# Decoder layer on one core: gate parts in one operand, windowed slot sums, offsets read a tile ahead, low parts moved to GpSimd

## What is computed

```python
x = x + self_attention(layernorm(x), Wq, Wk, Wv, Wr)        # 16 heads of 64, causal mask of -50
x = x + cross_attention(layernorm(x), ctx, w_q, w_k, w_v, w_o)
x = x + ffn(layernorm(x), w_in, w_out, w1, w2, wg, we, gb, eb)

# ffn, flat = [2048, 256]
shared = (silu(a) * b) @ w_out.T            with a, b = split(flat @ w_in.T)      # 512 each
g_probs = softmax(flat @ wg.T + gb)         # 2 groups, the likelier one is taken
e_probs = softmax over the 4 experts of that group of (flat @ we.T + eb)
topv, topi = top_k(e_probs * g_prob, 2)     # two experts per token
h = silu(a1) * b1                           with a1, b1 = split(flat @ w1.T)
out = shared + sum over the two experts e of weight_e * (h @ w2[e].T)
```

## Time and profile before

| what | us |
| --- | --- |
| median of 3 runs (741.8 to 742.43) | 741.85 |
| the profiled execution | 741.35 |
| its span in the profile | 739.6 |
| TensorE busy | 732.7 |
| VectorE busy | 459.8 |
| ScalarE busy | 443.6 |
| GpSimd busy | 309.3 |

### The profile page before, as it was taken

One profiled execution on the slowest core, in us unless ns is written; L12 is line 12 of the kernel. 1 busy time (PEld: TensorE's weight loads), 2 busy tenths in 40 slices (PEclk: granted clock), 3 DMA queues, 4 the chain that ended last, 5 costly groups with the idle time before them and its releaser, 6 DMA issues.

```text
span 739.6 us, 17762 instructions
## 1 busy us (share of the span) xinstructions
PE 732.7 (99%) x6371; PEld 641.1 (87%) x6371; DVE 459.8 (62%) x951; ACT 443.6 (60%) x1473; POOL 309.3 (42%) x336
## 2 busy tenths in 40 slices
PE   8999999999999999999999999999999999999998
PEld 7888888888888888888888888888878889999987
DVE  6777767767667865564565555456767746444277
ACT  5876566665666778765656666657834534555322
POOL 2655225222423657363253226324660772445400
PEclk9999999999999999999999999999999999999999
DMA  6799600000000012000000000200050555777271
GB/s 200 239 372 203 229 1 0 0 0 0 0 0 1 29 63 82 2 29 3 1 0 28 0 0 17 96 0 2 30 228 1 200 200 176 236 210 210 69 274 66
DMA packets 35962, 64.68 MB, mean 87 GB/s; under 512 B 7972, under 2 KB 15652, under 8 KB 35332
## 3 DMA queue, kind: packets, MB, share of 16 engines
q1 hardware_dynamic: 31188, 50.17, 22.0%
q0 software_dynamic: 4432, 13.54, 4.9%
q10 hardware_dynamic: 288, 0.26, 0.1%
HBM read 38.06 MB, written 30.09 MB: 92 GB/s over the span
## 4 chain that ended last, share of the span: by engine, by line
PE 98%; ACT 0%; DVE 0%; POOL 0%; issue 0%; POOLq 0%; DVEq 0%
PE psW L150 15%; PE psW L152 14%; PE psW L151 14%; PE psW L927 8%; PE psT L913 5%; PE psT L150 4%; PE psT L152 4%; PE psT L151 4%; PE psS L981 4%; PE psA L981 4%; PE psS L150 4%; PE psS L152 3%; PE psS L151 3%; PE psA L152 2%; PE psA L151 2%; PE psA L150 2%
## 5 line engine op out<-in xcount | busy, mean ns | idle before, releaser
L530 POOL TENSOR_TENSOR prob<-prob,rsum 128x512 f32<-128x512 f32 x128 | 134.7, 1054 | 284.2 <-DVE rsum L777 284.2
L633 ACT ACTIVATE prob<-psA,nmin 128x128 f32<-128x128 f32 x256 | 91.8, 384 | 1.3
L633 ACT ACTIVATE prob<-psS,nmin 128x128 f32<-128x128 f32 x256 | 90.4, 376 | 1.9 <-DVE nmin L772 1.9
L608 ACT ACTIVATE oT_hi<-psW 128x512 fp32r<-128x512 f32 x63 | 37.7, 598 | 88.2 <-PE psW L927 88.2
L604 ACT ACTIVATE pT<-psT 128x512 f32<-128x512 f32 x64 | 38.3, 599 | 52.9 <-PE psT L913 52.0
L777 DVE RECIPROCAL rsum<-psums 128x4 f32<-128x4 f32 x128 | 21.9, 171 | 68.3 <-ACT prob L633 68.1
L927 PE MATMUL psW<-pT,v 128*64 128x128 f32 x1008 | 62.3, 276 | 0.0
L760 DVE COPY kt<-psW 128x512 f32<-128x512 f32 x57 | 39.3, 689 | 36.3 <-PE psW L152 36.3
L927 PEld LDWEIGHTS psW<-pT,v 128*64 128x64 f32 x1008 | 54.4, 137 | 6.6 <-issue 3.1
L753 DVE TENSOR_TENSOR oT_lo<-psW,oT_hi 128x512 fp32r<-128x512 f32 x63 | 43.2, 686 | 26.0 <-ACT oT_hi L608 25.8
L633 ACT ACTIVATION_READ_ACCUMULATOR prob<-psA,nmin 128x1 f32 x256 | 57.6, 225 | 0.0
(11 more groups left out here) (388 smaller groups left out, 2186.5 us busy)
## 6 DMA issues: line engine op xcount, KB each, us to landing
stage<-hs SPq DMA_DIRECT2D x39, 257.0 KB, 3.0
hs<-empty SPq DMA_DIRECT2D x1, 9984.0 KB, 35.3
w_lo<-w_raw SPq DMA_DIRECT2D x4, 1024.0 KB, 7.8
w_hi<-yt SPq DMA_DIRECT2D x4, 1024.0 KB, 9.4
stage<-ctxT SPq DMA_DIRECT2D x4, 512.0 KB, 4.1
xres<-x SPq DMA_DIRECT2D x3, 512.0 KB, 8.3
out<-xres SPq DMA_DIRECT2D x12, 128.0 KB, 2.0
stage<-wv SPq DMA_DIRECT2D x2, 512.0 KB, 4.6
```

The costliest lines, as they stand in the source:

```text
L530: nc.gpsimd.tensor_tensor(prob[i][:, r, :], prob[i][:, r, :], rsum[i][:, r].unsqueeze(2).broadcast_to([P, TPG, P]), ALU.mult).then_inc(pro ...
L633: e = nc.scalar.activation(prob[i][:, n, :], flat(psX[i][:])[:, n * P:(n + 1) * P], ACT.Exp, bias=nmin[i][:, n:n + 1], scale=-1.0, accum_o ...
```

## The change

- `WARM` goes from 10 to 8.
- The gate weights' high and low parts stand side by side in one operand of 20 columns. `gate_logits` multiplies it with the high part and the low part of z: 2 matmuls per half of the width in place of 3. The two halves of the 20 rows go through bias (the lower ones get a bias of 0, set by a memset on GpSimd, for which SyncE's queue waits) and transposes, and are added by VectorE, which now reads PSUM twice. The product of low by low parts, left out before, is made.
- The first gate product goes to psT and no longer waits for the residual; the two banks of the values that follow change places; its bias copy on ScalarE stands ahead of the last two exponentials.
- The z transposes of the third group move ahead of the last projection.
- `slot_counts` moves behind H10 and multiplies with sums of `sel` over four tiles, made by two VectorE additions (`windows`): 4 matmuls in place of 16.
- VectorE's product of unit H8 moves into `gate_ranks`; those of H9, H10, H11 each move one place up among the routing steps.
- `BEHIND` becomes S11: S10 runs ahead of the expert tiles, in psA.
- The offset of the next tile is loaded in the middle of a tile, behind its sixth product; the turn of the tile after next stands behind its first product. The high-by-high product comes first.
- The low parts of S10 to S23 are made by GpSimd, behind its scatters.

```diff
-WARM = 10
+WARM = 8
...
+        FIRST_LOGITS, LOGITS_0, LOGITS_1 = psT[:, 0, :], psW[:, 0, :], psW[:, 1, :]
...
             for k in range(KT):
-                mm = product(psW[0:NG, bank, :], (gws[0][:, k, :], gws[1][:, k, :]), (z_g[0][:, k, :], z_g[1][:, k, :]),
-                             k == 0, k == KT - 1)
+                for n_part, part in enumerate(z_g):
+                    mm = nc.tensor.matmul(bank[0:2 * NG, :], gw[:, k, :], part[:, k, :], start=k == 0 and n_part == 0,
+                                          stop=k == KT - 1 and n_part == 1)
...
                             exps(p, 0, range(4, 8))
-                            exps(p, 1, range(0, 8))
+                            exps(p, 1, range(0, 6))
                             act.wait_ge(slots_zero, 32)
-                            gate_bias(act, 0, above, 0)
+                            gate_bias(act, 0, above, FIRST_LOGITS)
+                            exps(p, 1, range(6, 8))
...
+                for name in UNITS[BEHIND - 1:]:
+                    m = int(name[2])
+                    pool.wait_ge(h_hi, S_UNITS.index(name) + 1)
+                    nc.gpsimd.tensor_tensor(hids[1][:, m, :], silu_of(UNITS.index(name)), hids[0][:, m, :].bitcast(F32),
+                                            ALU.subtract).then_inc(h_lo, 1)
...
+                def windows():
+
+                    dve.wait_ge(sel_done, 2)
+                    nc.vector.tensor_tensor(two_tiles, sel_behind[:, 1:, :].bitcast(F32), sel_behind[:, 0:WINDOW - 2 + B, :].bitcast(F32),
+                                            ALU.add).then_inc(windowed, 1)
+                    dve.wait_ge(windowed, 1)
+                    nc.vector.tensor_tensor(four_tiles, two_tiles[:, 2:, :], two_tiles[:, 0:B, :], ALU.add).then_inc(windowed, 1)
...
-                dve.wait_ge(gate_copied, 1)
+                dve.wait_ge(gate_copied, 2)
                 dve.wait_ge(ffn_consts, 4)
                 gate_maxima(0)
-                gate_ranks(0, between=3)
+                gate_ranks(0, between=3, later=4)
+                windows()
                 unselected()
                 last_choices()
-                unit(4)
+                unit(5)
                 slots()
-                unit(5)
+                unit(6)
                 slot_experts()
-                unit(6)
+                unit(7)
                 slot_weights()
-                unit(7)
...
-                    for t in range(B):
-                        mm = nc.tensor.matmul(slots_ps[:, t + 1:B + 1, :], ones[:],
-                                              sel[:, t, :].unsqueeze(1).broadcast_to([P, B - t, NE]), start=False,
-                                              stop=t == B - 1, skip_group_check=True)
+                    pe.wait_ge(windowed, 2)
+                    for t in range(0, B, WINDOW):
+                        mm = nc.tensor.matmul(slots_ps[:, t + 1:B + 1, :], ones[:], four_tiles[:, 0:B - t, :], start=False,
+                                              stop=t == B - WINDOW, skip_group_check=True)
...
+                gate_logits(pe, 0, z_of[ORDER[0]], FIRST_LOGITS)
                 pe.wait_ge(res_done, STEPS - 3)
-                gate_logits(pe, 0, z_of[ORDER[0]], 0)
+                weighted_values(pe, STEPS - 4, 0, PAIRS - 4, psW[:, 0, :])
...
-                gate_logits(pe, 1, z_of[ORDER[1]], 1)
+                gate_logits(pe, 1, z_of[ORDER[1]], LOGITS_1)
+                z_transposes(pe, L0 + 2, Z_IN_T)
                 pe.wait_ge(oT_lo, STEPS)
                 out_project(pe, PAIRS - 2, 0, psW[:, 0, :])
                 pe.wait_ge(gate_biased, 2)
                 out_project(pe, PAIRS - 2, 1, psW[:, 1, :])
-                z_transposes(pe, L0 + 2, Z_IN_T)
...
-                unit("H10", slot_counts)
+                unit("H10")
+                slot_counts()
...
                     for k in range(HT):
-                        mm = product(Y_BANKS[i % BUFS], (hT(0, i)[:, k, :], hT(1, i)[:, k, :]),
-                                     tuple(w[:, k, bass.ds(offset, D)] for w in w2s), k == 0, k == HT - 1)
+                        hi, lo = (hT(n, i)[:, k, :] for n in range(2))
+                        rows_hi, rows_lo = (w[:, k, bass.ds(offset, D)] for w in w2s)
+                        nc.tensor.matmul(bank, hi, rows_hi, start=k == 0, stop=False)
+                        if k == 0 and 0 < i < NT - 2:
+                            turn(i + 2)
+                        nc.tensor.matmul(bank, lo, rows_hi, start=False, stop=False)
+                        mm = nc.tensor.matmul(bank, hi, rows_lo, start=False, stop=k == HT - 1)
+                        if k == 1 and i + 1 < NT:
+                            following = offset_of(i + 1)
                     mm.then_inc(y_mm, 1)
+                    return following
...
+                offset = offset_of(0)
+                turn(2)
                 for i in range(NT):
-                    if i + 2 < NT:
-                        turn(i + 2)
-                    if i == 1:
-                        pe.wait_ge(h_done, BEHIND)
-                    expert(i, offset_of(i))
+                    offset = expert(i, offset)
```

More of the change, by code:

```diff
@@ L305, in gate_bias @@
             act.wait_ge(gate_mm, n + 1)
-            nc.scalar.activation(dst[0:NG, :], psW[0:NG, bank, :], ACT.Identity, bias=gbias[:, 0:1]).then_inc(gate_biased, 1)
+            nc.scalar.activation(dst[0:2 * NG, :], bank[0:2 * NG, :], ACT.Identity, bias=gbias[:, 0:1]).then_inc(gate_biased, 1)
         def gate_transposes(pe, n, src):
@@ L323, in build @@
         graw = sb("graw", [P, KT, NG])
-        gbias = sb("gbias", [NG, 1])
-        gws = [sb(f"gw_{n}", [P, KT, NG], F32R) for n in ("hi", "lo")]
+        gbias = sb("gbias", [2 * NG, 1])
+        gw = sb("gw", [P, KT, 2 * NG], F32R)
+        gw_hi, gw_lo = gw[:, :, 0:NG], gw[:, :, NG:2 * NG]
         PIECES = [f"{w} {half}" for w, half in
@@ L513, in attention_gpsimd @@
             def attention_gpsimd(pool):
+                nc.gpsimd.memset(gbias[:], 0.0).then_inc(bias_zero, 1)
                 nc.gpsimd.memset(ident[:], 0.0).then_inc(zeroed, 1)
@@ L1215, in build @@
             UNITS = [f"H{T}" for T in H_ORDER] + [f"S{g}{m}" for g in S_ORDER for m in range(HT)]
-            BEHIND = UNITS.index("S10")
+            BEHIND = UNITS.index("S11")
             S_UNITS = [n for n in UNITS if n[0] == "S"]
@@ L1425, in gate_maxima, with gate_ranks @@
                     link(nc.vector.tensor_tensor(le, le, wide(emax[:, tiles], PER_GROUP), ALU.subtract))
-                def gate_ranks(r, between=None):
+                def gate_ranks(r, between, later):
                     tiles, _, _, pg, pe4 = of_round(r)
@@ L1453, in gate_ranks @@
                                                  wide(coef_, PER_GROUP), ALU.mult))
-                    if between is not None:
-                        unit(between)
+                    unit(between)
                     linked()
@@ L1464, in gate_ranks @@
                         [P, n * GROUPS, PER_GROUP, PER_GROUP]), ALU.mult))
+                    unit(later)
                     linked()
@@ L1482, in logits_copy @@
                     dve.wait_ge(gate_T, NGRP)
-                    first, behind = ROUND[r][0], ROUND[r][-1] + 1
-                    nc.vector.tensor_copy(flat(logits[:, first:behind, :]),
-                                          psW[:, 1, first * NG:behind * NG]).then_inc(gate_copied, 1)
+                    parts = psW[:, 1, 0:B * 2 * NG].rearrange("p (t n) -> p t n", n=2 * NG)
+                    nc.vector.tensor_copy(logits[:], parts[:, :, NG:2 * NG]).then_inc(gate_copied, 1)
+                    dve.wait_ge(gate_copied, 1)
+                    nc.vector.tensor_tensor(logits[:], parts[:, :, 0:NG], logits[:], ALU.add).then_inc(gate_copied, 1)
                 def unit(u):
@@ L1619, in rest_vector @@
                         ln_tile(L0 + 3, 3, t)
+                nc.vector.memset(sel_behind[:, 0:WINDOW - 1, :].bitcast(F32), 0.0).then_inc(sel_done, 1)
                 dve.wait_ge(z_done, (L0 + 3) * TPG)
@@ L1680, in rest_vector @@
                 add_shared(0)
-                for name, n in (("S11", 2), ("S12", 2), ("S13", 2), ("S20", 5), ("S21", 2), ("S22", 2), ("S23", 1)):
-                    u = UNITS.index(name)
-                    unit(u)
-                    split(UNITS[u - 1])
+                for name, n in (("S12", 2), ("S13", 3), ("S20", 5), ("S21", 3), ("S22", 2), ("S23", 1)):
+                    unit(UNITS.index(name))
                     for _ in range(n):
@@ L1698, in unit @@
                         pe.wait_ge(h_done, last_user(u) + 1)
+                    if u == BEHIND - 1:
+                        pe.wait_ge(shared_added, 2)
                     if u >= BEHIND:
@@ L1820, in expert @@
                 def expert(i, offset):
+                    bank = Y_BANKS[i % BUFS]
+                    following = None
                     pe.wait_ge(hT_lo, i + 1)
```

62 lines of the change are left out of this document (33 added, 29 removed).

## The result

The changed kernel takes **745.32 us** (median of 6 runs, 744.78 to 746.0) against 742.12 for the kernel before beside it (6 runs, 741.8 to 742.43): ratio 1.0046, 95% interval 1.0036 to 1.0056. I had said 738.9 and faster; it is slower by 3.4 us (3.2 by the medians alone). The profiled execution took 744.92 around a span of 743.2, 3.6 more than the 739.6 before.

The account below looks back on a forecast made before the run. TensorE, busy 99% of the span, was taken as the bound. Start -0.4, last step and routing -0.25, tiles -2.45, tail 0 sum to -3.1, of which 2.95 kept: median 738.9 us, range 736.2 to 741.4.

Parts of the forecast that it names:

- Start and last step: Warm-up through first products, -0.4; last attention step with gate and routing, direct savings 3.6 against new waits 3.4, -0.25.
- the waits I gave as 1.05, 1.8 and 0.55: New TensorE waits in the last step: second group's z transposes, third group's z transposes, low part at third gate product.
- the five slot products: Routing on TensorE: 5 products at 0.11 for 17, -1.25, with no wait for VectorE's window sums, by 0.2.
- The first rival: Last step: the two z waits cost 1.5 together, not 2.85; 736 to 737.5 us; chance 0.13.
- Tail: Units behind the tiles: low parts on GpSimd at 1.05 each, VectorE freed of 8 x 0.6; total effect 0.
- Loads of rows: Before the tiles: first load issued at 618.3, landing at 621.3, first turn at 622.55, so no wait.
- Tiles: Expert tiles: 1.85 us each from loading offsets earlier, -2.0, and -0.45 at the last three; together -2.45.
- The third rival: Expert tiles gain nothing because the sequencer's unchanged work per tile is the bound; 741 us; chance 0.15.
- The second rival: Expert tiles: the mid-tile load starves TensorE at the seventh product, +3.7 over 38 tiles; about 745 us; chance 0.09.
- the queue of 64: Expert tiles: by this TensorE queue length tiles run at product rate, term -3.1 instead of -2.45, median 738.2.

Follow-up runs that it names:

- z_back: Changed kernel with the third group's z transposes behind the last out-projection again: 742.99 us, ratio 1.0022 to the kernel before.
- best_padded: Changed kernel with z transposes back, late low parts on VectorE, fewer adds before the last two units, gate bias after all exponentials, 32 unused bytes: 737.99 us, ratio 0.9955.
- the pad: Changed kernel with 32 unused bytes per partition behind the joined gate operand, so later tensors start on multiples of 64 again: ratio 1.0035 to the kernel before.
- one_offset: Changed kernel with the offset loaded once ahead of the tiles, every tile using the first tile's expert: 745.05 us, ratio 1.0052 to the kernel before.

## Why the prediction was wrong

**Start and last step: right.** -0.37 and -0.16 against -0.4 and -0.25, the first a guess (half of a bound) that came true. The first gate product went 0.5 ahead, the waits I gave as 1.05, 1.8 and 0.55 are 1.27, 1.74 and 0.72 (the gap between two matmuls' starts, less the 0.23 that they lie apart anyway), the five slot products take 0.47 and wait for nothing. The first rival, that these waits would be shorter, fell. z_back shows that the second and third could be had back, for a new wait of 0.4, and best_padded brings the first from 1.10 to 0.65.

**Tail: the step that failed.** I wrote "Nothing gained, nothing lost: **0**"; it is +3.1 and +0.5. The sum had VectorE reach the last unit's product 0.5 earlier; it reached it 2.8 later (35.19 us behind the end of the tiles, where 35.13 less the 2.78 of S10 had been). Four things are wrong in it. I freed VectorE of 8 x 0.6 and did not charge it for GpSimd's operations beside its adds; of the 5.5 that it was freed of, it lost 5.1 again. I took 1.05 for a low part from a row of another operation, a multiplication by a broadcast column; the subtraction takes 1.29 with VectorE idle, and up to 1.46 beside its adds. A nearer row stood in the trace of before: GpSimd's subtractions of 128x1024 take 2.4 there, so half of that, 1.2. And by the page that I had set beside the sum it was 1.3. Third, I never costed the adds: with S10 ahead of the tiles the sixteen pairs are spread behind six products instead of seven, three of them ahead of S22's in place of two. Fourth, I gave GpSimd's closing DRAIN no cost: behind a low part it ends the program, +0.5. I had named the contention, from a page, and kept it out of the sum because a row was at hand.

**Loads of rows: late.** Forecast: issue at 618.3, first turn with 1.2 to spare. Measured, on GpSimd and SyncE's queue and TensorE:

```profile
574.09 1.22 POOL L1299 DMA_INDIRECT hs<-stage,slot  x1 [17.53 <-DVE stage L1517]
577.20 1.86 POOL L1299 DMA_INDIRECT hs<-stage,slot  x1 [0.30 <-issue]
585.10 1.63 POOL L1299 DMA_INDIRECT hs<-stage,slot  x1 [0.30 <-DVE z L1517]
...
621.19 2.22 SPq L1265 DMA_DIRECT2D stage<-hs  x5
...
623.98 1.42 PE L1842 MATMUL psW<-ident,stage 128*128 128x128 f32 x8
```

The scatters start 2.59 later (I had 1.8; 0.57 is what the attention groups had lost by then); then the 32 take 47.1 to the load and not 45.0: three of them need 1.86, 1.42 and 1.63, each started while VectorE was in a 1024-wide operation with two SBUF inputs (1.22 us). Each ends 0.84 to 0.85 behind that operation. In the kernel before the scatters happened to start ahead of those or near their end, and behind the first two none took over 1.18. "GpSimd's scatters follow at their own pace" was wrong: VectorE's order sets it. All nine runs with the new routing order show these three, none of the five with the old. Of the +0.78, about 0.3 is the wait for the load and 0.45 the memory's place; the +0.41 is the rest of the wait.

**Tiles: mechanism right, size off.** The last three tiles gave what I took. In the middle I forecast 1.85, it is 1.879: the sequencer, which I had as "nearly as long at it", needs 1.89. The products' 0.003 more (place) doesn't show in it, since with the pad the 36 tiles take the same. The third rival named this bound ("the sequencer's work per tile is unchanged and is the bound"), and its 741 would have been near without the tail. The second rival, a load that starves TensorE in mid-tile, occurs, but with 0.02 to 0.08 a tile; its 745 is the measured time by chance, for its +3.7 in the tiles is -1.6. From the queue of 64 of the Trainium skill, "TensorE: Matmul & The Clock Gate", section "Architectural detail", I had worked out tiles at their product rate: that is what one_offset shows, and only without the load.

**Place in memory: not in the prediction at all.** +0.4 in the units, and perhaps 0.4 of the attention's +0.94; the tiles didn't pay for it.

## What to carry to other kernels

Work moved from VectorE to GpSimd has to be charged twice where VectorE's neighbouring operations read two SBUF inputs: there the two engines take turns, and nothing is relieved; put it beside operations that read PSUM. And let GpSimd end early: here its closing DRAIN ended some 7.2 us behind the start of its last operation. Before moving an operation ahead on TensorE, subtract when its operand is ready; before pulling a unit out of a stage, count what VectorE still has to do under the units that remain. Last, compare stretches that the edit didn't touch: if they change their pace, look where the tensors lie.

## What I had not expected of the hardware

- Moving the weights 32 bytes off a multiple of 64 slows some stretches of fp32 products by 2% (a unit 2.80 us in place of 2.75) and leaves others at 2.72. The shift alone costs the kernel before 0.9 us (ratio 1.0012, 1.0003 to 1.0021); the pad's gain in the changed kernel (1.0046 to 1.0035) is within the intervals.
- An add of 0.48 us beside a GpSimd operation of 1.29 takes 1.53 and ends 0.28 behind it; GpSimd's own, 1.29 alone, takes up to 1.46 when started during an add.
- GpSimd's closing DRAIN takes 7.1 to 7.8 us from its last operation on. Where that was a low part begun 6.2 to 7.0 us ahead of SyncE's last instruction, it ended the program, up to 0.9 us late.
- TensorE's sequencer was the bound of a stage in which TensorE reads as busy all the time: 1.89 us for twelve products at computed addresses, four transposes, one load of a register and the waits. Taking only the load out brings 1.86, TensorE's own pace.
- GpSimd's indirect scatters are held up by VectorE's wide two-input operations: 0.97 us became 1.42 to 1.86.
